# 32-head attention on Trainium2: four heads' scores on their own 32 rows, and one normalisation per batch

## The reference, cut to what matters

```python
q = (hidden_state @ Wq + bq).reshape(b, l, KVH, GROUPS, HD).transpose(0, 2, 3, 1, 4)   # KVH 8, GROUPS 4, HD 16
k = (encoder_hidden_state @ Wk + bk).reshape(b, s, KVH, HD).transpose(0, 2, 1, 3)
v = (encoder_hidden_state @ Wv + bv).reshape(b, s, KVH, HD).transpose(0, 2, 1, 3)
scores = jnp.einsum('bkgld,bksd->bkgls', q, k) * scale + encoder_attention_mask[:, :, None, :, :]
attn = jax.nn.softmax(scores, axis=-1)
out = jnp.einsum('bkgls,bksd->bkgld', attn, v)
x = out.transpose(0, 3, 1, 2, 4).reshape(b, l, H) @ Wo + bo + hidden_state
return (x - mean(x)) * rsqrt(var(x) + EPS) * gamma + beta
```

## Time and profile before

| what | value |
|---|---|
| median of three runs (lowest, highest) | 3483.05 us (3481.4, 3486.6) |
| the profiled execution's own time | 3478.85 us |
| its span in the trace | 3476.9 us |
| busy: PE, PE's weight loads, DVE, ACT, POOL | 91%, 71%, 61%, 42%, 22% |

### The profile page before, as it was taken

How to read it: one execution, slowest core, us unless ns; L and a number is a source line. 1 busy time by engine, 2 the same in 40 slices (tenths; PEclk the granted TensorE clock), 3 DMA queues, 4 the chain that set the end, 5 groups by cost and what they waited for, 6 DMA issues and landing times.

```text
span 3476.9 us, 55755 instructions
## 1 busy us (share of the span) xinstructions
PE 3160.6 (91%) x18176; PEld 2472.0 (71%) x18176; DVE 2108.5 (61%) x5496; ACT 1469.5 (42%) x4209; POOL 761.3 (22%) x532
## 2 busy tenths in 40 slices
PE   7999999996799999868999999999999679999986
PEld 6666555675688888768555555599999668888875
DVE  2888888854888888833355544511100488888883
ACT  1777777764233333325344444432212223333332
POOL 1111112001444444410010010000000244444441
PEclk9999999998899999979999999999999889999987
DMA  2000000021322222310000000030000332322231
GB/s 104 22 22 30 21 21 22 3 115 41 96 84 82 82 84 81 91 59 24 18 27 17 17 17 26 1 134 0 0 0 1 127 95 82 86 81 81 83 91 41
DMA packets 96363, 183.17 MB, mean 53 GB/s; under 512 B 10138, under 2 KB 87514, under 8 KB 92862
## 3 DMA queue, kind: packets, MB, share of 16 engines
q1 hardware_dynamic: 96190, 181.21, 16.4%
HBM read 171.27 MB, written 9.90 MB: 52 GB/s over the span
## 4 chain that ended last, share of the span: by engine, by line
PE 58%; issue 16%; DVE 13%; ACT 5%; POOL 3%; DMA 2%; DVEq 1%; SPq 1%; ACTq 0%; POOLq 0%
PE psum L467 14%; PE psum L272 10%; PE psum L1336 7%; PE psum L1398 5%; PE psum L1281 5%; PE psum L1299 4%; PE psum L1344 3%; DVE psum L662 2%; DVE arena L1505 2%; POOL arena L1048 2%; PE psum L458 2%; PE psum L248 2%; DVE arena L671 1%; ACT arena L1633 1%; PE psum L481 1%
## 5 line engine op out<-in xcount | busy, mean ns | idle before, releaser
L467 PE MATMUL psum<-arena 128*128 128x200 f32 x4096 | 814.8, 361 | 110.0 <-POOL arena L1035 75.2
L467 PEld LDWEIGHTS psum<-arena 128*128 128x128 f32 x4096 | 766.5, 208 | 192.0 <-issue 102.0
L1633 ACT ACTIVATE arena<-arena 100x361 f32<-100x361 f32 x768 | 460.2, 599 | 463.5 <-DVE arena L1494 458.8
L1336 PE MATMUL psum<-arena 128*100 128x361 f32 x1536 | 609.2, 478 | 17.3 <-DVE arena L1494 14.7
L1048 POOL TENSOR_TENSOR arena<-arena 128x800 f32<-128x800 f32 x256 | 445.8, 1741 | 721.9 <-DVE psum L662 721.8
L1494 DVE CUSTOM_DVE_ANT_0 arena<-psum,arena 100x361 f32<-100x361 f32 x768 | 406.4, 529 | 311.0 <-issue 306.2
L671 DVE TENSOR_TENSOR_SCAN arena<-arena,psum 128x808 f32<-128x808 f32 x256 | 470.2, 1837 | 91.3 <-PE psum L458 74.9
L1344 PEld LDWEIGHTS psum<-arena 100*128 100x128 f32 (+1 forms) x2304 | 301.6, 151 | 245.3 <-issue 124.0
L1676 POOL TENSOR_TENSOR arena<-arena 128x400 f32<-128x400 f32 x192 | 167.8, 907 | 1185.1 <-PE psum L1336 971.5
L272 PE MATMUL psum<-arena 128*128 128x200 f32 (+1 forms) x2048 | 352.6, 335 | 21.8 <-DMA arena<-L_w 19.9
L272 PEld LDWEIGHTS psum<-arena 128*128 128x128 f32 x2048 | 349.8, 191 | 22.8 <-DMA arena<-L_w 19.9
(11 more groups left out here) (102 smaller groups left out, 3415.8 us busy)
## 6 DMA issues: line engine op xcount, KB each, us to landing
arena<-v_rows SPq DMA_DIRECT2D x512, 202.0 KB, 3.2
arena<-ctxT SPq DMA_DIRECT2D x32, 722.0 KB, 4.1
arena<-L_w SPq DMA_DIRECT2D x8, 1152.0 KB, 15.9
arena<-L_w SPq DMA_DIRECT2D x8, 1024.0 KB, 11.0
v_rows<-arena SPq DMA_DIRECT2D x32, 202.0 KB, 2.1
arena<-L_fc SPq DMA_DIRECT2D x4, 1024.0 KB, 8.5
arena<-L_pj SPq DMA_DIRECT2D x4, 1024.0 KB, 16.0
arena<-xT SPq DMA_DIRECT2D x4, 800.0 KB, 9.5
```

What stands on the lines that cost most here:

```text
L467: mm = pe.matmul(chunk(bank, j), m.W[n][:, k, c * P:(c + 1) * P], src[:, k, :], start=k == 0, stop=k == C - 1)
L1336: pe.matmul(bank[k % 2][0:L, 0:S], q, kT[u][:, 0 if gqa else nl, :], start=True, stop=True).then_inc(scores_ready.sem, 1)
L1633: act.activation(pr[k % 8][0:L], sm[k % 4][0:L], ACT.Exp, bias=nmx[0:L, k:k + 1], scale=-1.0, accum_out=den[0:L, k:k + 1]).then_inc(exp_re ...
```

## The change

L0 gets a function of its own, `gqa_attention()`; L2 keeps `attention()`. Per step q it now treats a **quad** of four heads, 16 quads a turn, 8 a batch:

- The four heads of a quad belong to the four pairs of key/value heads. Rows 32n to 32n+31 hold pair n, and the queries are masked by parity only (two masks instead of eight): head n's scores come from a matmul over the 32 rows 32n to 32n+31, into bank n. The four matmuls are issued one behind the other.
- Nothing is divided per head. The sums of a whole batch are inverted at once, POOL repeats them 16 times each, PE spreads them to the rows and columns of the output, ACT copies that out, and one multiplication per batch on DVE joins them to the weighted sums. The bias of the values is added when they are copied (with weights that sum to one it is the same).
- The probabilities are padded to 384 columns, so that each transpose is copied by one instruction instead of two. ACT copies heads 0 and 2 of a quad (bank 4), DVE heads 1 and 3 (bank 7): one bank each, four before. There are two buffers of transposed probabilities of 16 heads each.
- The transposes of a quad stand one quad behind its scores, two before the projections and two behind them. The weighted sum of 16 heads is cut into three parts for three quads. The values of a batch come in its own quads 2 to 4, the keys of the next batch in quads 5 to 7.
- The mask is negated on POOL instead of DVE.

```diff
+        def spread_reciprocals(t, u, last):
+            pe.wait_ge(rden_repeated.sem, rden_repeated.at(t, 2 * u + 2))
...
+            for g in range(4):
+                mm = pe.matmul(bank[6][:, g * L:(g + 1) * L], rden_rows[0:L, g].rearrange("l n o d -> l (n o d)"),
+                               ident[0:L, 0:L], start=True, stop=True)
...
+            def transposes(pair):
...
+                for n in pair:
+                    h = 4 * (q - 1) + n
+                    pe.wait_ge(exp_ready.sem, exp_ready.at(t, h + 1))
+                    if h >= 2 or not first:
+                        if n % 2 == 0:
+                            pe.wait_ge(copied_by_act.sem, copied_by_act.at(t, h // 2))
+                        else:
+                            pe.wait_ge(copied_by_dve.sem, copied_by_dve.at(t, h // 2))
+                    for j in range(3):
+                        mm = pe.transpose(bank[4 + 3 * (n % 2)][:, j * L:(j + 1) * L], pr[h % 8][0:L, j * P:(j + 1) * P],
+                                          ident[0:L, 0:L])
...
+            if q < QUADS:
+                if q % 8 == 0:
+                    pe.wait_ge(q_masked.sem, q_masked.at(t, 2 * u + 2))
+                    pe.wait_ge(k_ready.sem, k_ready.at(t, u + 1))
+                if q or not first:
+                    pe.wait_ge(scores_masked.sem, scores_masked.at(t, 4 * q))
+                for n in range(4):
+                    a = slice(32 * n, 32 * n + 32)
+                    pe.matmul(bank[n][0:L, 0:S], qm[u][a, o, g, :], kT[u][a, :], start=True,
+                              stop=True).then_inc(scores_ready.sem, 1)
+            if q % 4 in (2, 3, 0):
+                m, j = ((q + 2) // 4 - 2, (q + 2) % 4)
+                if there(4 * m, first):
+                    weighted(t, m, j)
+            transposes((0, 1))
+            if q % 8 == 1 and there(q - 8, first):
+                spread_reciprocals(t, q // 8 - 1, last)
+            if q < QUADS:
+                if q % 8 == 2:
+                    values(t, u, 0, first)
...
+                    if q % 8 == 5:
+                        keys(t, u + 1, (0, 1))
+                    if q % 8 == 6:
+                        keys(t, u + 1, (2,))
+                    if q % 8 == 7:
+                        keys(t, u + 1, (3,))
+            transposes((2, 3))
...
+            masked_scores(0)
+            masked_scores(1)
+            masked_scores(2)
+            copy(1)
+            masked_scores(3)
+            copy(3)
...
+            if q % 8 == 4:
+                if q < QUADS:
+                    values(t, u)
+                if there(q - 12, first):
...
+                    dve.tensor_tensor(qT[:, :, bass.ds(t * (2 * L) + (u - 1) * L, L)],
+                                      bank[5][:, 0:4 * L].rearrange("p (h l) -> p h l", h=4),
+                                      spread_rden.rearrange("p (h l) -> p h l", h=4),
+                                      ALU.mult).then_inc(attention_ready.sem, 1)
...
+            exponential(0)
+            exponential(1)
+            copy(0)
+            if q % 8 == 1 and there(q - 8, first):
...
+                act.activation(spread_rden, bank[6][:, 0:4 * L], ACT.Copy).then_inc(rden_spread.sem, 1)
+            exponential(2)
+            exponential(3)
+            copy(2)
+            if q < QUADS and q % 8 == 7 and not (last and u):
+                keys(t, u + 1)
```

More of the change, by code:

```diff
@@ L168, in program @@
             if n % 2 == 0:
-                stack.append(attention(core, f"L{n}", after))
+                stack.append((attention if n else gqa_attention)(core, f"L{n}", after))
             else:
@@ L1745, in constants @@
     red[p, 24 + p % HC] = 1
-    hm = (p[:, None] // 16 == np.arange(8)[None]).astype(np.float32)
+    hm = np.zeros((P, 8), np.float32)
+    hm[:, 0:4] = np.stack([p // 16 % 2 == 0, p // 16 % 2 == 1, np.ones(P), -np.ones(P)], 1)
     qm = (p[:, None] // 32 == np.arange(4)[None]).astype(np.float32)
@@ L1760, in attention_weights @@
         vec[:, 9:13] = fc_b.reshape(C, C, P).transpose(2, 0, 1)
-    return pack([rows(q[:, q_perm]), rows(k), rows(v), rows(o[o_perm]), vec])
+    bv_rows = [np.broadcast_to(vectors[2], (P, len(vectors[2])))] if fc_b is None else []
+    return pack([rows(q[:, q_perm]), rows(k), rows(v), rows(o[o_perm]), vec] + bv_rows)
 GQA = np.arange(D).reshape(8, 4, 16).transpose(1, 0, 2).reshape(-1)
```

325 lines of the change are left out of this document (added).

## The result

The changed kernel takes 3366.12 us, the median of 4 runs (3360.1 to 3371.08). The kernel before, on the same chip, takes 3482.36 us (3481.4 to 3486.6). The ratio is 0.9666, interval 0.9654 to 0.9677. On a second chip it is 0.9646 (0.963 to 0.9662). The profiled execution is the one of 3360.1 us.

What follows compares the result with a forecast made beforehand. PE bound L0's attention, 37.3 of 40.7 us a batch; then a three-engine chain, 8 x 4.05 + 1.0 + 1.4 = 34.8. With the ends -90.6, clock +11: about -80 from 3483.05, 3403 us, range 3350 to 3480.

Steps and rivals of the forecast that it cites:

- Row tiles all at once: L0 scores on PE: the four heads' matmuls run together, 0.60 us a quad instead of 2.4.
- the forecast's break-even: L0 attention: with row tiles one behind the other, slower than before once the mean quad is over 4.79 us.
- the chain through ACT's copy: L0 quad: no engine is full; second transposes wait for the first pair's copies and stand ahead of the next scores.
- The chain's length, 4.05 us: L0 quad: sum of the links from the last transposing matmul of one quad to that of the next.
- The 0.95 and the 0.16: Chain links: 0.95 us from scores start to mask-add start; 0.16 us from PE's weight load to its matmul.
- the 0.05: Chain link: 0.05 us from ACT's copy to PE.
- Quad 4 and the keys: Two places a batch: values and product on DVE in quad 4, +1.0 us; ACT's late key copy in quad 7, +1.4.
- The ends: L0 attention: first scores 2.7 us earlier, 7.5 us of work behind the last quad, end at 634.4 instead of 725.0.
- the clock term: PE's clock in L0's attention: 11 us allowed for falls at a third of the stage's 32 pauses.
- the bound of 0.95: Sign that the forecast is right: PE's clock in the stage at 0.95 or more.
- Rival 5, the looser chain: L0 quad: copies overlap neighbours, 3.7 us a quad, no clock term, 3350 us; no own chance, inside the main case's 61%.
- the main case: Row tiles overlap and the chain binds L0's quads; spans 3350 to 3450 us, rival 5 included, 61%.

Runs made afterwards that it cites:

- Experiment 5: Changed kernel with each head's scores from a matmul over all 128 rows, so no row tiles: 3506.34 us, ratio 1.0066.
- experiment 1: Changed kernel with ACT copying head 0's transpose ahead of exponential 1 instead of behind it: 3343.14 us, ratio 0.9597.
- experiment 9: Changed kernel with the two waits ahead of each DVE mask-add and each PE transpose in swapped order: 3378.04 us, ratio 0.9701.
- experiment 2: Changed kernel with ACT copying the next batch's keys behind its first copy of quad 7, not behind everything: 3338.37 us, ratio 0.9593.
- experiment 3: Changed kernel with DVE multiplying a batch's output one quad later than it copies the values: 3356.6 us, ratio 0.9642.
- kernel 10: The changed kernel without any edit, run again for comparison on the chip of experiment 9: 3360.11 us.
- experiment 6: Changed kernel with the scores of all four heads on the same rows 0 to 31: 3765.3 us, ratio 1.0813.
- experiment 7: Changed kernel with an extra DVE pass of 100x361 per head of L0, into unused memory: 3455.95 us, ratio 0.9925.
- experiment 12: Changed kernel with heads 0 and 1 on rows 0 to 31, heads 2 and 3 on rows 32 to 63: 3463.71 us, ratio 0.9945.

## Why the prediction was right, and what it had too large

The forecast was 3403 us with a range of 3350 to 3480; 3366 lies inside, on its low side. The mechanism was right, and the gain was put at 80 us where it was 116. Point by point:

- **Row tiles all at once: right.** That was read from column tiles and was the largest uncertainty. The union of eight matmuls is 0.87 us, and what they add to a quad 0.80, as the 0.60 with the changes of shape had it. Of this 0.385 lies between the two bunches of four, not 0.30. Experiment 5 shows the other end, 2.53, and the forecast's break-even: a mean quad of 42.1 / 8 = 5.26 us is slower than before, as it should be over 4.79. The Trainium skill, TensorE: Matmul & The Clock Gate, Part 3, gives 3.07x for four row tiles. Experiment 5 against the changed kernel gives 2.53 / 0.80 = 3.2 here, with the changes of shape in the 0.80, so the runs agree with it nearly.
- **The bound becomes the chain through ACT's copy: right.** The wait stands in the groups with 38.0 us, and experiment 1 moves it.
- **The chain's length, 4.05 us: too long by 0.295.** This is the term that was mis-sized. Its parts, forecast and measured in the loop: 0.09 + 0.17 + 0.95 from the last transposes to the mask-add against 0.18 + 0.89, 0.14 too long; from the copy's start to the transposes 0.61 against 0.45, 0.16 too long; the rest within 0.04. The 0.95 and the 0.16 were taken from the earlier trace rows, the first heads of the stage, which lie in the written-out turn; the 0.05 has no row. In its written-out turns the new kernel does take 3.95 (1.20 and 0.54 for these two parts), and experiment 9 shows why: in that code it costs 0.2 us that the wait which ends last is the second of two. The remaining 0.1 is mostly the copy's part, 0.61 against 0.54, where copy, handshake and weight load had been added up. The loop could have been read beforehand. One head of the kernel before in it, of which the first line is in the earlier trace rows:

```profile
299.61 0.77 PE L1336 MATMUL psum<-arena 128*100 128x361 f32 x2
...
300.42 0.53 DVE L1494 CUSTOM_DVE_ANT_0 arena<-psum,arena 100x361 f32<-100x361 f32 x1 [0.34 <-issue]
```

- Here the mask-add starts 0.81 us behind the scores, not 0.95; in that loop it is 0.81 or 0.90 nearly everywhere that DVE had been idle.
- **Quad 4 and the keys: right in place and nearly in size.** The step with values and product costs 0.75 more (1.0 forecast), the key stall 1.33 (1.4), both shown by experiments 2 and 3. It was one quad later in the count of scores, since DVE does them behind quad 4's mask-adds.
- **The ends.** First scores 72.7 us (71.5 forecast): the keys' first matmul already starts 1.1 us later than before (67.88 against 66.75). The projection ahead of it starts 0.3 later, within the 0.5 allowed for the weights, but also takes 0.9 longer; why wasn't looked into. The 127 quads from first to last scores took 518.1 us, against 551.4: 12 batches of the loop 2.6 us less each, -31, and the four written-out ones -2 together. What lies behind the last quad's scores took 15.5 us where 11.6 was forecast: 4.05 + 7.5. The clock falls at 598.6 us, and most of the spread of the reciprocals (L1213, which waits for POOL's repeat, L1514) and of the weighted sum (L1227) runs at 1.2 GHz, ahead of the product (L1394):

```profile
599.49 2.03 PE L1213 MATMUL psum<-arena 100*128 100x100 f32 x8 [2.09 <-POOL arena L1514]
601.45 4.19 PE L1227 MATMUL psum<-arena 128*32 128x400 f32 x24
605.72 0.57 DVE L1394 TENSOR_TENSOR arena<-psum,arena 128x400 f32<-128x400 f32 x1 [7.55 <-PE psum L1227]
```

- The sum of these is 1.2 - 33.3 + 3.9 = -28 us: 606.3 instead of 634.4. With the 11 us of the clock term, not needed in this execution, that is the 37 us by which the forecast was too high, but for 2 us between the profiled executions and the medians.
- **The clock: the allowance of 11 us wasn't needed in the profiled execution.** There it falls only at the start (13.7 us from 73.0) and twice at the end (585.0 and 598.6), not in the middle. That is the fastest of the four; the second profile, kernel 10, has one fall in the middle more, which costs 4.5 us. The fear wasn't empty: experiments 1, 6, 7, 9 and 12 lose the clock in the middle again and again. The mean of the stage, 0.98, is above the bound of 0.95 that was set. That the term came out near nothing in this execution, the forecast had no reason for.
- **Rival 5, the looser chain** (3.7 us a quad, 3350), described the loop better than the main sum, and it was inside the main case. Its reason (copies that overlap their neighbours) isn't what happened; the handshakes are shorter.
- PE was to be near 80% busy and is 86%, as the quads are shorter.

## What to carry to other kernels

Price a handshake from the same kind of code as the one it will run in: the written-out turn and the loop of this kernel differ by 0.2 us a quad, in two links of one chain. When two changes each relieve a different engine, price them together: apart they gave 28 and 26 us here (the 26 would be some 65 had the clock not fallen, by the estimate in experiment 7), together 116. Once no engine is full, look for what stands last on an engine's list though others wait for it; three such moves gave another 58 us.

## What the runs showed that was not expected

- **A busy PE can lose its clock.** With all scores on the same 32 rows PE was 98% busy and ran at 0.71, with no idle time at all ahead of many of the falls; over 128 rows it was 96% busy, paused 1.43 us a batch and ran at 1.00. These are one kernel each. Two sets of rows ran at 0.91 with the same pauses of 1.43 us, but four sets also fell in experiments 1, 7 and 9, so the runs don't show that the number of rows in use decides it.
- **Matmuls on another set of rows start ahead of older ones** that wait for their rows: in experiment 12 14 ns behind the first, while the older second one starts at 385 ns. The Trainium skill, TensorE: Matmul & The Clock Gate, Part 3, says that matmuls start and end in program order; the records of experiment 12 differ.
- **The order of two waits** ahead of an instruction changed the written-out plain quad from 3.955 to 3.753 us, and the one of the loop the other way, from 3.755 to 3.825.
- **The same code can hold or lose the clock** in one execution: experiment 1 at 0.88 for 210 us and at 1.00 for the next 240. What decides it stays open.
